# Two-layer cross-attention: the first batch's scores start ahead of the layer-1 weight preparation, which moves into that batch's layer 0

## The chip, the cores and the metric

The kernel runs on one core of a Trainium2 chip. The metric is the device time of one execution in microseconds; the time before is the median of three runs, 1359.41 us (1356.07 to 1359.81).

## The reference, cut to what matters

There are 16 batches. Each has 100 query rows `x` and 361 context rows `ctx_2048`, both 512 wide, all in float32. Two layers follow each other and both attend to the same context.

```
layer 0:  q = x@Wq + bq; k = ctx@Wk + bk; v = ctx@Wv + bv      # 32 query heads of 16, 8 key/value heads
          attn = softmax(q k^T / 4 + mask0)
          x = layernorm(attn v @ Wo + bo + x) * gamma + beta
layer 1:  a = layernorm(ctx) * ln_gamma + ln_beta              # mean and variance of each context row
          Q = x@Wq^T; K = a@Wk^T; V = a@Wv^T                   # 16 heads of 32
          attn = softmax(Q K^T / sqrt(32)), masked
          x = x + tanh(gate) * (attn V @ Wo^T)
```

The layer norm of the context is folded into the layer-1 weights: Wk and Wv of layer 1 are multiplied by ln_gamma, their column means are subtracted (centring), and the keys are then scaled by each context row's reciprocal deviation. ln_beta gives a bias per column. This folding is done once, before or during the first batch.

## The kernel before, in words

**Engines.** One block holds a program for each engine: SP issues all transfers in order on one queue, PE does matmuls and transposes, DVE, ACT and POOL the rest. They meet only through semaphores. Each program is written out by hand, so the order of the lines is the order of the work on that engine.

**A batch.** There are 48 heads in all, handled in 24 pairs p. Pairs 0 to 15 are layer 0, pairs 16 to 23 layer 1. For a head k, `score` (L387, L391) is one matmul into bank k % 3 of SCO, `shift` on DVE (L752) adds the mask and finds the row's minimum, `exps` on ACT (L962) makes the probabilities. The score of head k waits for the exponentials of head k - 3 (`prob` at least k - 2). Two pairs later `transpose_probs` (L401) transposes a pair into TP, and ACT (three of four pairs, L975) or DVE (one of four, L765) copies them to PT. `out_half` (L421, L426) multiplies with the values.

**Layer-1 keys and values of a batch** are spread between the pairs. `keys1` is 48 matmuls in four chunks m of twelve (weights in a high and a low part), into PJ. A chunk then goes by `keys1_scaled` on DVE (L744), an addition of the bias on POOL (L1130), `keys1_high` on ACT (L992), and a subtraction on POOL (L1133). SP stores it with `store_keys1` (L253) and, when two chunks are stored, reads them back in another layout with `load_keys1` (L260, four transfers into K1S). `keys1_high` of chunks 2 and 3 waits until the store of chunks 0 and 1 has landed. `values1` is 36 matmuls into PJ.

**What a batch loads for the next one.** At the head of its loop SP runs, in this order: `load_keys1(b, 0)`, the next batch's XT (L297), the next AT (L211), a wait for POOL's mask step (`mk1_a`), the mask MU (L303), the next batch's context rows into V1, also called NAT (L216, L218), and then `store_keys1` of chunks 2 and 3. POOL's mask step (L1157) stands behind `keys1_low(b, 2)` in POOL's program. DVE takes statistics of the next batch's context rows (`ctx_stats`, L730) in pair 9, behind its two shifts and `repeat_sums`, and in pair 10; its first one waits for the two row transfers (`l_nat`). V1 is then overwritten by the values of the batch, from ACT's pair 11.

**The prologue.** After layer-0 keys, queries and values of batch 0 (L350, L363, L380), PE does the layer-1 key bias (L499), the column means of the key weights (L504), the value bias (L509), the value weights' means (L515), and then 36 of the 48 `keys1` matmuls (`K1_AHEAD`). DVE centres the key weights (L823), makes their low part (L827), adds the layer-0 value bias (L721) and centres the value weights (L835). ACT makes the high parts (L1026, L1030) and POOL the low part of the value weights (L1149). Only then does `batch(0, True, True)` begin with the first score (L387), which waits for Q0S and K0S (L239, L245). The raw key weights lie in the first half of PT, the raw value weights in the second, so the first copies into PT wait for both low parts.

**Names that the change touches**: `WK1_raw`, `K1_STEPS`, `V1_STEPS`, `keys1_scaled`, `keys1_high`, `keys1_low`, and the order of SP, PE, DVE, ACT and POOL up to and in batch 0. Batches 1 to 15 keep their order.

Of the kernel before, what the change touches and what calls it, by code (L numbers as in the profile page):

```python
# [21 lines left out]
def two_layer_cross_attention(nc, x_rows, x_cols, ctx_rows, ctx_cols, mask0, mask1,  # L22
# [24 lines left out]
    with ExitStack() as ctx:  # L47
# [62 lines left out]
        YT = OT  # L110
        WK1_raw = PT_flat[:, 0:C * D].rearrange("p (c n) -> p c n", c=C)
        WV1_raw = PT_flat[:, WV1_AT:WV1_AT + C * D].rearrange("p (c n) -> p c n", c=C)
# [70 lines left out]
        K1_STEPS = {p: (i + K1_AHEAD, j + K1_AHEAD) for p, (i, j) in K1_LATE.items()}  # L183
        V1_STEPS = spans({3: 2, 4: 2, 5: 4, 8: 2, 9: 2, 10: 4, 11: 4, 12: 4, 13: 4, 14: 4, 15: 4})
        OUT1_STEPS = {6: (0, 2), 7: (2, 5), 8: (5, 8)}
        PV0_PARTS = {7: (0, 0, 2), 9: (0, 2, 3), 11: (1, 0, 2), 12: (1, 2, 3), 15: (2, 0, 2)}
# [22 lines left out]
        def _(sp):  # L209
# [61 lines left out]
            load_ctx_rows(0)  # L271
            sp.dma_start(PT_flat[:, 0:C * D], wk1.rearrange("p c n -> p (c n)")).then_inc(l_k1, 16)
            sp.dma_start(ROWS[:, :], rows.partition_broadcast(P)).then_inc(l_row, 16)
# [5 lines left out]
            sp.dma_start(MU[0:T, :], mask1[0].partition_broadcast(T)).then_inc(l_mk1, 16)  # L279
            sp.dma_start(R0[0:T, :], x_rows[0]).then_inc(l_xn, 16)  # L280
            for G in range(2):
                for j in range(NJ):
                    ct, jh = 2 * (j % 2) + G, j // 2
                    sp.dma_start(WO0[32 * ct:32 * ct + 32, 2 * jh:2 * jh + 2, :],
                                 wo0[32 * j:32 * j + 32, 2 * G:2 * G + 2, :]).then_inc(l_o, 16)
            sp.wait_ge(wk_c, C)
            sp.dma_start(WQ1[:, :, :], wq1).then_inc(l_o, 16)
            sp.wait_ge(wv_c, C)
# [51 lines left out]
        def _(pe):  # L340
# [162 lines left out]
            for c in range(C):  # L503
                last = pe.matmul(SCO[:, 0, :], ONES[:, :], WQ1[:, c, :], start=c == 0, stop=c == C - 1)  # L504
            last.then_inc(wk_cm, 1)
            pe.wait_ge(l_v1, 16)
            for m in range(C):
                for c in range(C):
                    last = pe.matmul(TP[:, 0, m:m + 1], WV1_raw[:, c, m * P:(m + 1) * P], B1[:, c:c + 1],  # L509
                                     start=c == 0, stop=c == C - 1)  # L510
            last.then_inc(kb_mm, 1)
            pe.wait_ge(wv_g, C)
            pe.wait_ge(k0_l, 1)
            for c in range(C):
                last = pe.matmul(SCO[:, 1, :], ONES[:, :], WO1[:, c, :], start=c == 0, stop=c == C - 1)  # L515
            last.then_inc(wv_cm, 1)
            pe.wait_ge(k1w_l, 1)
            for i in range(K1_AHEAD):
                if i == 3 * C:
                    pe.wait_ge(q0_l, 4)  # L520
                elif i == 6 * C:
                    pe.wait_ge(k1_f, 1)
                keys1(0, i)
            pe.wait_ge(wv_c, C)
            pe.wait_ge(kb_ev, 1)
            pe.wait_ge(vb_ev, 1)
            pe.wait_ge(rs_ev, 1)

# [6 lines left out]
            def values1_steps(b, first, p):  # L535
                for i in range(*V1_STEPS.get(p, (0, 0))):
# [12 lines left out]

            def batch(b, first, more):  # L550

                for p in range(L0P):
# [17 lines left out]
                    if p == 5 and not first:  # L570
                        pe.wait_ge(k1_f, 4 * b + 4)
                        sums_transposed(b - 1, 2)
                    keys1_steps(b, p)
                    values1_steps(b, first, p)
                    if p in OUT1_STEPS and not first:
                        if p == 6:
                            pe.wait_ge(attn, 3 * b)
                        out1(b - 1, range(*OUT1_STEPS[p]))
# [114 lines left out]
        def _(dve):  # L693
# [61 lines left out]
            def probs_out(b, p):  # L755
                dve.wait_ge(pt_mm, NPAIR * b + p + 1)
                h = p // 4
                if p == 1 and isinstance(b, int) and b == 0:
                    dve.wait_ge(k1w_l, 1)
                if p == 5 and isinstance(b, int) and b == 0:  # L760
                    dve.wait_ge(v1w_l, 1)
                if p % 4 == 1:

                    wait_from(dve, pv, NHALF * b + h - 1)
                dve.tensor_copy(PT[0:SP, h % 2, 2 * (p % 4):2 * (p % 4) + 2, :], TP[0:SP, :, 0:SC * T]).then_inc(pt_dve, 1)  # L765
# [52 lines left out]
            keys0_low(0)  # L818
            queries0_low(0)
            dve.wait_ge(kb_mm, 1)  # L820
            dve.wait_ge(wk_cm, 1)
            for c in range(C):
                dve.scalar_tensor_tensor(out=WK1_raw[:, c, :], in0=SCO[:, 0, :], scalar=-1.0 / D,  # L823
                                         in1=WQ1[:, c, :], op0=ALU.mult, op1=ALU.add)\
                    .then_inc(wk_c, 1)
            dve.wait_ge(k1w_h, 1)
            dve.tensor_tensor(flat(WK1l), PT_flat[:, 0:C * D], flat(WK1h).bitcast(F32), ALU.subtract)\  # L827
                .then_inc(k1w_l, 1)
            dve.wait_ge(pool_zero, 3)
            dve.wait_ge(l_row, 16)  # L830
            values0(0, SCO[:, 2, :])
            dve.wait_ge(wv_cm, 1)
            dve.wait_ge(kb_mm, 2)
            for c in range(C):
                dve.scalar_tensor_tensor(out=WV1_raw[:, c, :], in0=SCO[:, 1, :], scalar=-1.0 / D,  # L835
                                         in1=WO1[:, c, :], op0=ALU.mult, op1=ALU.add)\
                    .then_inc(wv_c, 1)
            dve.wait_ge(l_rp, 16)
            dve.tensor_copy(RP[:, :, :], SX[:, 0:2, :]).then_inc(rep_id, 1)
# [101 lines left out]
        def _(act):  # L941
# [23 lines left out]
            def probs_out(b, p):  # L965
                act.wait_ge(pt_mm, NPAIR * b + p + 1)
                h = p // 4
                if p == 0 and isinstance(b, int) and b == 0:
                    act.wait_ge(k1w_l, 1)
                if p == 4 and isinstance(b, int) and b == 0:  # L970
# [51 lines left out]
            act.wait_ge(kb_mm, 2)  # L1022
            act.activation(KB[:, :], TP[:, 1, 0:C], ACT.Copy).then_inc(kb_ev, 1)
            act.activation(VBC[:, :], TP[:, 0, 0:C], ACT.Copy).then_inc(vb_ev, 1)
            act.wait_ge(wk_c, C)
            act.activation(flat(WK1h), PT_flat[:, 0:C * D], ACT.Copy).then_inc(k1w_h, 1)  # L1026
            act.wait_ge(pad_zero, 3)
            rstd_out(0)
            act.wait_ge(wv_c, C)
            act.activation(flat(WV1h), PT_flat[:, WV1_AT:WV1_AT + C * D], ACT.Copy).then_inc(v1w_h, 1)  # L1030
            keys1_high(0, 0, True)
            keys1_high(0, 1, True)

            def batch(b, first, more):
                for p in range(L0P + 1):
# [12 lines left out]
                    if p == 13:  # L1048
                        unit_sums(b, 0, 2 * T)
                    if p == 2:  # L1050
                        keys1_high(b, 2, first)
                    elif p == 5:
                        keys1_high(b, 3, first)
                    elif p == 11:
# [53 lines left out]
        def _(pool):  # L1108
# [19 lines left out]
            def keys1_low(b, m):  # L1128
# [103 lines left out]
```

## Time and profile before

| | |
|---|---|
| median of 3 runs | 1359.41 us |
| profiled execution | 1352.98 us |
| its span, first to last instruction | 1351.2 us |
| PE busy | 1224.0 us, 91% of the span |
| PE weight loads | 904.3 us, 67% |
| DVE busy | 766.1 us, 57% |
| ACT busy | 766.0 us, 57% |
| POOL busy | 272.9 us, 20% |
| mean granted TensorE clock | 0.973 |
| DMA | 153.75 MB, mean 114 GB/s |
| sizes in KB: one K1S load, four transfers of | 364 |
| XT; AT; MU | 200; 722; 35.3 |
| context rows of one batch, two transfers | 484 and 238 |
| one store of a key chunk | 364 |

The durations come from the one profiled execution, whose time is 1352.98 us; it is 1.8 us over its span and 6.4 us below the median. An engine counts as busy while it has an instruction that moves data; waits, branches and the issue of transfers are not busy time. A row's bracket gives how long the engine was idle ahead of it and who ended that.

### The profile page before, as it was taken

Reading aid. Unit: us, or ns where it says so; the run is one execution under the profiler, and the core shown is the slowest. Engines: PE = TensorE matmul, PEld = TensorE weight load, DVE = VectorE, ACT = ScalarE, POOL = GpSimd, SP = SyncE. Lnnn points to the kernel's source line nnn. Section 1 sums busy time; section 2 is a strip of 40 time slices with the busy share of each in tenths; the row PEclk is TensorE's granted clock in tenths of the full one; section 3 lists DMA queues with packets and bytes.
Section 4 is the critical chain, followed back from the end, with each engine's and each line's share of the span. In section 5 each row is a group of like instructions: output and inputs, shape, how many; then the busy total and the mean of one; then the engine's idle time right before and its main releaser. Section 6 shows DMA issues by size and latency. Waiting matters only on the chain.

```text
span 1351.2 us, 31567 instructions
## 1 busy us (share of the span) xinstructions
PE 1224.0 (91%) x9768; PEld 904.3 (67%) x9768; DVE 766.1 (57%) x2289; ACT 766.0 (57%) x2179; POOL 272.9 (20%) x280
## 2 busy tenths in 40 slices
PE   4899999999999899999989999999999999999967
PEld 4666676766767667676767667677666766766645
DVE  3465646656564666556566555656656566665533
ACT  3374647566464755637475564746647465664634
POOL 2311112121221312122131211213121121212100
PEclk8899999999999999999999999999999999999986
DMA  7753735255372635537163463616347361643500
GB/s 231 192 130 89 179 65 153 70 126 131 81 178 57 161 73 112 141 76 182 51 158 76 109 156 74 172 47 158 92 93 172 74 168 44 147 110 87 129 0 7
DMA packets 77820, 153.75 MB, mean 114 GB/s; under 512 B 10384, under 2 KB 47056, under 8 KB 77152
## 3 DMA queue, kind: packets, MB, share of 16 engines
q1 hardware_dynamic: 77792, 153.40, 46.8%
q8 instruction: 15, 0.25, 0.1%
q14 instruction: 13, 0.11, 0.0%
HBM read 113.72 MB, written 39.65 MB: 114 GB/s over the span
## 4 chain that ended last, share of the span: by engine, by line
PE 71%; issue 10%; DVE 8%; ACT 7%; DMA 2%; POOL 1%; DVEq 1%; ACTq 0%; SPq 0%; POOLq 0%
PE PJ L350 16%; PE TP L401 13%; PE SCO L387 7%; PE OA L421 5%; PE PJ L451 5%; PE SCO L624 5%; PE PJ L363 4%; PE SCO L443 4%; ACT PR L962 3%; PE SCO L391 3%; PE OA L426 3%; ACT PT L975 1%; DVE SCO L752 1%; PE SCO L350 1%; POOL YRS L1169 1%
## 5 line engine op out<-in xcount | busy, mean ns | idle before, releaser
L962 ACT ACTIVATE PR<-SCO,MN 100x361 f32<-100x361 f32 x768 | 426.6, 566 | 206.9 <-DVE MN L752 205.3
L752 DVE CUSTOM_DVE_ANT_0 SCO<-SCO,MK 100x361 f32<-100x361 f32 x768 | 398.2, 553 | 223.0 <-PE SCO L387 169.9
L401 PE MATMUL TP<-ident,PR 100*128 100x100 f32 x2304 | 269.5, 253 | 9.0 <-ACT PT L975 7.0
L401 PEld LDWEIGHTS TP<-ident,PR 100*128 100x128 f32 x2304 | 237.5, 143 | 58.5 <-ACT PT L975 15.6
L975 ACT ACTIVATE PT<-TP 121x600 f32<-121x600 f32 x288 | 194.4, 675 | 86.4 <-PE TP L401 84.8
L962 ACT ACTIVATION_READ_ACCUMULATOR PR<-SCO,MN 100x1 f32 x768 | 158.1, 206 | 0.0
L387 PE MATMUL SCO<-K0S,Q0S 64*100 64x362 f32 x512 | 130.2, 411 | 5.9 <-ACT PR L962 5.9
L765 DVE COPY PT<-TP 121x600 f32<-121x600 f32 x96 | 75.2, 783 | 104.4 <-PE TP L401 103.5
L391 PE MATMUL SCO<-K1S,Q1S 128*100 128x362 f32 x256 | 94.1, 402 | 23.3 <-ACT PR L962 18.5
L752 DVE DVE_READ_ACCUMULATOR2_ANT MN<- 100x1 f32 x768 | 108.8, 142 | 0.0
L451 PE MATMUL PJ<-WO,OT 128*100 128x256 f32 x256 | 70.4, 412 | 27.7 <-DVE OT L787 27.7
L350 PE MATMUL PJ<-TH,WK1h 128*128 128x364 f32 x256 | 93.9, 367 | 1.2 <-DVE WK1l L827 0.9
L1133 POOL TENSOR_TENSOR K1HL<-K1F,K1HL 128x364 fp32r<-128x364 f32 x64 | 61.6, 963 | 157.2 <-ACT K1HL L992 153.4
L421 PE MATMUL OA<-PT,V0P 121*32 121x200 f32 x1536 | 91.5, 350 | 0.8 <-ACT PT L975 0.8
L387 PEld LDWEIGHTS SCO<-K0S,Q0S 64*100 64x100 f32 x512 | 55.2, 161 | 48.8 <-ACT PR L962 15.4
L350 PE MATMUL PJ<-WV1h,TH 128*121 128x512 f32 x192 | 80.9, 422 | 6.7 <-DVE R L794 6.7
L350 PE MATMUL PJ<-TL,WK1h 128*128 128x364 f32 x256 | 86.2, 337 | 0.0
L350 PE MATMUL PJ<-TH,WK1l 128*128 128x364 f32 x256 | 84.3, 329 | 0.0
L1130 POOL TENSOR_TENSOR K1F<-K1F,KB 128x364 f32<-128x364 f32 x64 | 50.9, 795 | 154.0 <-DVE K1F L744 154.0
L350 PE MATMUL PJ<-WV1h,TL 128*121 128x512 f32 x192 | 81.9, 426 | 0.0
L350 PE MATMUL PJ<-WV1l,TH 128*121 128x512 f32 x192 | 81.6, 425 | 0.0
L1163 POOL TENSOR_TENSOR R<-R,ROWS 100x512 f32<-100x512 f32 x16 | 20.6, 1288 | 278.5 <-DMA R<-x_rows 278.5
(138 smaller groups left out, 1781.9 us busy)
## 6 DMA issues: line engine op xcount, KB each, us to landing
K1S<-k_scr SPq DMA_DIRECT2D x128, 364.0 KB, 6.2
k_scr<-K1HL SPq DMA_DIRECT2D x64, 364.0 KB, 2.5
Q0S<-q_scr SPq DMA_DIRECT2D x128, 100.0 KB, 3.9
K0S<-k_scr SPq DMA_DIRECT2D x64, 182.0 KB, 4.9
AT<-ctx_cols SPq DMA_DIRECT2D x16, 722.0 KB, 9.4
V<-ctx_rows SPq DMA_DIRECT2D x16, 484.0 KB
q_scr<-QHL SPq DMA_DIRECT2D x16, 400.0 KB, 2.5
k_scr<-KHL SPq DMA_DIRECT2D x32, 182.0 KB, 3.0
```

The source lines that it names most:

```text
L350: return pe.matmul(dst, w, x, start=start and term == 0, stop=stop and term == 2)
L387: pe.matmul(dst, Q0S[64 * G:64 * G + 64, j, 2 * gh + gl, :], K0S[64 * G:64 * G + 64, j, 0:SE], start=True, stop=True).then_inc(scored, 1)
L391: pe.matmul(dst, Q1S[:, j, m, :], K1S[:, j, m, 0:SE], start=True, stop=True).then_inc(scored, 1)
L401: last = pe.transpose(TP[:, k % 2, c * T:(c + 1) * T], PR[0:T, k % NPR, c * SP:c * SP + P], ident[0:T, 0:T])
L421: last = pe.matmul(OA[32 * j:32 * j + 32, 0:2 * T], lhs, rhs, start=gh == 0 and c == 0, stop=gh == 1 and c == SC - 1)
L451: last = pe.matmul(PJ[0:T, 1, cols], OT[:, c, :], WO1[:, c, cols], start=c == 0, stop=c == C - 1)
L624: last = pe.matmul(SCO[:, 1, m * T:(m + 1) * T], WQ1[:, c, m * P:(m + 1) * P], YT[:, c, :], start=c == 0, stop=c == C - 1)
L752: dve.tensor_tensor_reduce(out=bank, in0=bank, in1=mask[0:T, :], scale=scale, scalar=3.4e38, op0=ALU.add, op1=ALU.min, accum_out=MN[0:T, k ...
L765: dve.tensor_copy(PT[0:SP, h % 2, 2 * (p % 4):2 * (p % 4) + 2, :], TP[0:SP, :, 0:SC * T]).then_inc(pt_dve, 1)
L962: act.activation(PR[0:T, k % NPR, 0:S], SCO[0:T, k % 3, 0:S], ACT.Exp, bias=MN[0:T, k:k + 1], scale=-1.0, accum_out=SM[0:T, k:k + 1]).then ...
L975: act.activation(PT[0:SP, h % 2, 2 * (p % 4):2 * (p % 4) + 2, :], TP[0:SP, :, 0:SC * T], ACT.Copy).then_inc(pt_act, 1)
L1133: pool.tensor_tensor(K1HL[:, m % 2, 1, :], K1F[:, :], K1HL[:, m % 2, 0, :].bitcast(F32), ALU.subtract).then_inc(k1_l, 1)
```

## The change

The raw key weights go to WO0, so the first half of PT is free at once; WO0's own eight loads move behind the key weights' low part, and WQ1's load goes ahead of them. The means go to PJ and not to SCO. The first scores are issued right after the key weights' means. Value bias, value means, low parts, all 48 key matmuls and their scaling, high and low parts come between the pairs of batch 0. Cut to its core:

```diff
-        WK1_raw = PT_flat[:, 0:C * D].rearrange("p (c n) -> p c n", c=C)
+        WK1_raw = WO0
+        FIRST_K1_STEPS = spans({2: 7, 3: 7, 4: 7, 5: 7, 6: 7, 7: 7, 8: 6})
+        FIRST_V1_STEPS = spans({9: 6, 10: 6, 11: 6, 12: 6, 13: 6, 14: 4, 15: 2})
 # SP
+            sp.wait_ge(wk_c, C)
+            sp.dma_start(WQ1[:, :, :], wq1).then_inc(l_o, 16)
+            sp.wait_ge(k1w_l, 1)
             for G in range(2):
                 for j in range(NJ):
...
-            sp.wait_ge(wk_c, C)
-            sp.dma_start(WQ1[:, :, :], wq1).then_inc(l_o, 16)
             sp.wait_ge(wv_c, C)
             sp.dma_start(WO1[:, :, :], wo1).then_inc(l_o, 16)
             store_keys1(0, 0)
 # PE
-                last = pe.matmul(SCO[:, 0, :], ONES[:, :], WQ1[:, c, :], start=c == 0, stop=c == C - 1)
+                last = pe.matmul(PJ[:, 0, :], ONES[:, :], WQ1[:, c, :], start=c == 0, stop=c == C - 1)
             last.then_inc(wk_cm, 1)
...
-            pe.wait_ge(k1w_l, 1)
-            for i in range(K1_AHEAD):
...
+            def first_keys1_steps(p):
+                for i in range(*FIRST_K1_STEPS.get(p, (0, 0))):
+                    if i == 0:
+                        pe.wait_ge(k1w_l, 1)
+                    elif i == 3 * C:
+                        pe.wait_ge(wv_c, C)
+                    elif i == 6 * C:
+                        pe.wait_ge(k1_f, 1)
+                    elif i == 9 * C:
+                        pe.wait_ge(k1_f, 2)
+                    keys1(0, i)
...
-                    keys1_steps(b, p)
+                    if first:
+                        first_keys1_steps(p)
+                    else:
+                        keys1_steps(b, p)
                     values1_steps(b, first, p)
+                    if first and p == 0:
+                        values1_bias()
+                    elif first and p == 1:
+                        pe.wait_ge(q0_l, 4)
+                        values1_means()
+                    elif first and p == 2:
+                        pe.wait_ge(kb_ev, 1)
+                        pe.wait_ge(vb_ev, 1)
+                        pe.wait_ge(rs_ev, 1)
 # DVE: values0 and the copy to RP now stand ahead of the centring of the key weights
-                if p == 1 and isinstance(b, int) and b == 0:
-                    dve.wait_ge(k1w_l, 1)
-            keys1_scaled(0, 0)
-            keys1_scaled(0, 1)
...
-                    if p == 0:
+                    if first and p in (4, 6, 8, 10):
+                        keys1_scaled(b, p // 2 - 2)
+                    elif not first and p == 0:
                         keys1_scaled(b, 2)
-                    elif p == 4:
+                    elif not first and p == 4:
                         keys1_scaled(b, 3)
                     for k in (2 * p, 2 * p + 1):
                         shift(b, k)
+                    if first and p == 0:
+                        keys1_weights_low()
+                    elif first and p == 1:
+                        values1_centred()
 # ACT: the high part of the key weights stays ahead of the first exponentials
-            keys1_high(0, 0, True)
-            keys1_high(0, 1, True)
...
-                    if p == 2:
-                        keys1_high(b, 2, first)
-                    elif p == 5:
-                        keys1_high(b, 3, first)
+                    if first and p == 1:
+                        act.wait_ge(kb_mm, 2)
+                        act.activation(VBC[:, :], TP[:, 0, 0:C], ACT.Copy).then_inc(vb_ev, 1)
+                    elif first and p == 3:
+                        act.wait_ge(wv_c, C)
+                        act.activation(flat(WV1h), PT_flat[:, WV1_AT:WV1_AT + C * D], ACT.Copy).then_inc(v1w_h, 1)
+                    elif first and p in (5, 7, 9, 11):
+                        keys1_high(b, (p - 5) // 2, first)
+                    elif not first and p == 2:
+                        keys1_high(b, 2, first)
+                    elif not first and p == 5:
+                        keys1_high(b, 3, first)
 # POOL
-            keys1_low(0, 0)
-            keys1_low(0, 1)
             pool.wait_ge(v1w_h, 1)
             pool.tensor_tensor(flat(WV1l), PT_flat[:, WV1_AT:WV1_AT + C * D], flat(WV1h).bitcast(F32), ALU.subtract)\
                 .then_inc(v1w_l, 1)
+            keys1_low(0, 0)
+            keys1_low(0, 1)
```

## Rows read from the trace of the kernel before

**Rows 1.** The page's chain that ended last, share of the span, by engine.
```profile
PE 71%; issue 10%; DVE 8%; ACT 7%; DMA 2%; POOL 1%; DVEq 1%; ACTq 0%; SPq 0%; POOLq 0%
```

**Rows 2.** PE's timeline, 40 to 100 us: start, duration, [idle before, releaser].
```profile
40.89 3.63 PE L509 MATMUL TP<-COLS,PT 128*128 128x1 f32 x32
44.38 3.68 PE L515 MATMUL SCO<-WO,ONES 128*128 128x512 f32 x8
48.97 0.43 PE L350 MATMUL PJ<-TH,WK1h 128*128 128x364 f32 x1 [0.91 <-DVE WK1l L827]
...
55.12 0.41 PE L387 MATMUL SCO<-K0S,Q0S 64*100 64x362 f32 x2
55.86 0.43 PE L350 MATMUL PJ<-TH,WK1h 128*128 128x364 f32 x1 [0.34 <-DVE K1F L744]
...
60.17 0.62 PE L387 MATMUL SCO<-K0S,Q0S 64*100 64x362 f32 x1 [2.88 <-ACT PR L962]
...
81.63 0.41 PE L387 MATMUL SCO<-K0S,Q0S 64*100 64x362 f32 x2
...
83.35 0.40 PE L350 MATMUL PJ<-WV1h,TH 128*121 128x512 f32 x1
...
99.22 1.22 PE L421 MATMUL OA<-PT,V0P 121*32 121x200 f32 x24
```

**Rows 3.** Stretches of 4 us: engines' busy us, granted clock, DMA share, GB/s.
```profile
60.00:64.00 4.00, 3.83 (x11) 2.73 (x12) 1.91 (x7) 2.35 (x10) 3.48 (x2) 0.50 0.60 148
64.00:68.00 4.00, 4.00 (x21) 2.68 (x19) 2.08 (x7) 2.96 (x10) 2.62 (x3) 0.67 1.04 210
68.00:72.00 4.00, 3.50 (x22) 2.36 (x20) 2.69 (x10) 2.91 (x9) 1.48 (x2) 1.00 1.05 286
72.00:76.00 4.00, 3.21 (x35) 1.99 (x33) 2.54 (x9) 3.75 (x12) 1.50 (x2) 1.00 0.91 250
```

**Rows 4.** DVE's timeline, 40 to 80 us, same columns as rows 2.
```profile
41.16 2.48 DVE L823 SCALAR_TENSOR_TENSOR PT<-SCO,WQ 128x512 f32<-128x512 f32 x4 [17.39 <-PE SCO L504]
46.62 2.29 DVE L827 TENSOR_TENSOR WK1l<-PT,WK1h 128x2048 fp32r<-128x2048 f32 x1 [2.97 <-ACT WK1h L1026]
...
49.30 2.47 DVE L835 SCALAR_TENSOR_TENSOR PT<-SCO,WO 128x512 f32<-128x512 f32 x4
...
79.24 0.69 DVE L730 BATCH_NORM_STATS2 CST<-V 121x6 f32<-121x512 f32 x1
```

**Rows 5.** POOL's timeline, 55 to 66 us, same columns.
```profile
57.30 0.95 POOL L1133 TENSOR_TENSOR K1HL<-K1F,K1HL 128x364 fp32r<-128x364 f32 x1 [0.62 <-ACT K1HL L992]
58.21 4.52 POOL L1149 TENSOR_TENSOR WV1l<-PT,WV1h 128x2048 fp32r<-128x2048 f32 x1
62.68 0.80 POOL L1130 TENSOR_TENSOR K1F<-K1F,KB 128x364 f32<-128x364 f32 x1
```

**Rows 6.** SP's timeline of issues, 35 to 67 us: start, time to issue.
```profile
35.31 0.88 SPq L245 DMA_DIRECT2D K0S<-k_scr  x2
...
60.82 1.76 SPq L260 DMA_DIRECT2D K1S<-k_scr  x4
...
63.15 0.59 SPq L211 DMA_DIRECT2D AT<-ctx_cols  x1
...
66.51 0.37 SPq L218 DMA_DIRECT2D V<-ctx_rows  x1
```

**Rows 7.** Issue to landing: K0S, 20 to 60 us; then AT issued at 63.15.
```profile
DMA to landing us min/median/max: 4.2/4.6/5.5
...
DMA to landing us min/median/max: 11.7/11.7/11.7
```

**Rows 8.** The page's groups of an exponential: busy, mean ns of one.
```profile
L962 ACT ACTIVATE PR<-SCO,MN 100x361 f32<-100x361 f32 x768 | 426.6, 566 | 206.9 <-DVE MN L752 205.3
...
L962 ACT ACTIVATION_READ_ACCUMULATOR PR<-SCO,MN 100x1 f32 x768 | 158.1, 206 | 0.0
```

**Rows 9.** The page's transfers by form: count, KB each, median us to landing.
```profile
k_scr<-K1HL SPq DMA_DIRECT2D x64, 364.0 KB, 2.5
```

More of the change, by code:

```diff
@@ L271, in _ @@
             load_ctx_rows(0)
-            sp.dma_start(PT_flat[:, 0:C * D], wk1.rearrange("p c n -> p (c n)")).then_inc(l_k1, 16)
+            sp.dma_start(WK1_raw[:, :, :], wk1).then_inc(l_k1, 16)
             sp.dma_start(ROWS[:, :], rows.partition_broadcast(P)).then_inc(l_row, 16)
@@ L503, in _, with values1_bias, values1_means @@
             for c in range(C):
-                last = pe.matmul(SCO[:, 0, :], ONES[:, :], WQ1[:, c, :], start=c == 0, stop=c == C - 1)
+                last = pe.matmul(PJ[:, 0, :], ONES[:, :], WQ1[:, c, :], start=c == 0, stop=c == C - 1)
             last.then_inc(wk_cm, 1)
-            pe.wait_ge(l_v1, 16)
-            for m in range(C):
-                for c in range(C):
[L509 to L516, printed above, removed]
-            pe.wait_ge(k1w_l, 1)
-            for i in range(K1_AHEAD):
[L519 to L527, printed above, removed]
+            def values1_bias():
+                pe.wait_ge(l_v1, 16)
+                for m in range(C):
+                    for c in range(C):
+                        last = pe.matmul(TP[:, 0, m:m + 1], WV1_raw[:, c, m * P:(m + 1) * P], B1[:, c:c + 1],
+                                         start=c == 0, stop=c == C - 1)
+                last.then_inc(kb_mm, 1)
+            def values1_means():
+                pe.wait_ge(wv_g, C)
+                for c in range(C):
+                    last = pe.matmul(PJ[:, 1, :], ONES[:, :], WO1[:, c, :], start=c == 0, stop=c == C - 1)
+                last.then_inc(wv_cm, 1)
+            def first_keys1_steps(p):
[9 more added lines that the diff above has]
+                    keys1(0, i)
             def keys1_steps(b, p):
@@ L535, in values1_steps @@
             def values1_steps(b, first, p):
-                for i in range(*V1_STEPS.get(p, (0, 0))):
+                for i in range(*(FIRST_V1_STEPS if first else V1_STEPS).get(p, (0, 0))):
                     if i == 0:
@@ L819, in _ @@
             queries0_low(0)
+            dve.wait_ge(pool_zero, 3)
+            dve.wait_ge(l_row, 16)
+            values0(0, SCO[:, 2, :])
+            dve.wait_ge(l_rp, 16)
+            dve.tensor_copy(RP[:, :, :], SX[:, 0:2, :]).then_inc(rep_id, 1)
             dve.wait_ge(kb_mm, 1)
@@ L822, in _, with keys1_weights_low, values1_centred @@
             for c in range(C):
-                dve.scalar_tensor_tensor(out=WK1_raw[:, c, :], in0=SCO[:, 0, :], scalar=-1.0 / D,
+                dve.scalar_tensor_tensor(out=WK1_raw[:, c, :], in0=PJ[:, 0, :], scalar=-1.0 / D,
                                          in1=WQ1[:, c, :], op0=ALU.mult, op1=ALU.add)\
                     .then_inc(wk_c, 1)
[L826 to L839, printed above, removed]
-            keys1_scaled(0, 0)
-            keys1_scaled(0, 1)
+            def keys1_weights_low():
+                dve.wait_ge(k1w_h, 1)
+                dve.tensor_tensor(flat(WK1l), flat(WK1_raw), flat(WK1h).bitcast(F32), ALU.subtract)\
+                    .then_inc(k1w_l, 1)
+            def values1_centred():
+                dve.wait_ge(wv_cm, 1)
+                dve.wait_ge(kb_mm, 2)
+                for c in range(C):
+                    dve.scalar_tensor_tensor(out=WV1_raw[:, c, :], in0=PJ[:, 1, :], scalar=-1.0 / D,
+                                             in1=WO1[:, c, :], op0=ALU.mult, op1=ALU.add)\
+                        .then_inc(wv_c, 1)
             def batch(b, first, more):
@@ L967, in probs_out @@
                 h = p // 4
-                if p == 0 and isinstance(b, int) and b == 0:
-                    act.wait_ge(k1w_l, 1)
                 if p == 4 and isinstance(b, int) and b == 0:
@@ L1021, in _ @@
                     .then_inc(wv_g, 1)
[L1022 to L1026, printed above, removed]
             act.wait_ge(pad_zero, 3)
             rstd_out(0)
-            act.wait_ge(wv_c, C)
-            act.activation(flat(WV1h), PT_flat[:, WV1_AT:WV1_AT + C * D], ACT.Copy).then_inc(v1w_h, 1)
-            keys1_high(0, 0, True)
-            keys1_high(0, 1, True)
+            act.wait_ge(kb_mm, 1)
+            act.activation(KB[:, :], TP[:, 1, 0:C], ACT.Copy).then_inc(kb_ev, 1)
+            act.wait_ge(wk_c, C)
+            act.activation(flat(WK1h), flat(WK1_raw), ACT.Copy).then_inc(k1w_h, 1)
             def batch(b, first, more):
@@ L1049, in batch @@
                         unit_sums(b, 0, 2 * T)
-                    if p == 2:
+                    if first and p == 1:
[7 more added lines that the diff above has]
+                    elif not first and p == 2:
                         keys1_high(b, 2, first)
-                    elif p == 5:
+                    elif not first and p == 5:
                         keys1_high(b, 3, first)
-                    elif p == 11:
+                    if p == 11:
                         if more:
```

## The prediction
> **What bounds the kernel now.** I read the chain of waits first: PE holds 71% of it [rows 1], so what counts is when PE gets its next work. Then PE's timeline of the first 100 us, because nothing after batch 0's layer 0 is edited. The reader is to see there that PE is already full between the key means and the first score: the gap of 0.91 us ahead of the first key matmul is the only one from 40.9 to the score at 55.12 [rows 2]. Work that is moved behind the scores is therefore not removed. What is empty is short: 0.91, 0.34 and 2.88 us in these rows, and two gaps of 0.50 and 0.79 further on; 5.4 us in all. After the 2.88 us idle ahead of 60.17 the granted clock is 0.50 of full in 60 to 64 us and 0.67 in 64 to 68, that is 1.2 GHz for most of 6.6 us, with PE busy all that time [rows 3]: 3.0 us lost of at most 3.3. The most that the change can give is 5.4 + 3.0 = 8.4 us. Last I read SP's issues and the DMA rate, since the order of the key chunks sets when SP may go on.
>
> **The change, part by part.**
>
> The scores. The key means end where DVE's centring starts, 41.16 [rows 4]. K0S's last issue is at about 35.8 [rows 6] and lands 4.2 to 5.5 us later, 40.0 to 41.3 [rows 7]. So scores 0 and 1 stand at 41.2, 14 us earlier. The work in those 14 us comes back between the pairs: value bias 3.63, value means 3.68 [rows 2], 36 key matmuls in the 6.1 us from 48.97 to 55.12. Bank PJ for SCO costs nothing: PJ has no other use there. WO0 as the landing place costs nothing: its own loads go out at about 48 and are wanted at 100.
>
> Pairs 0 to 9. DVE centres to 43.6, shifts 0 and 1, waits for ACT's high part (2.97 us after the centring [rows 4]; two small copies are no longer in it, so 2.0) and makes the low part, 2.29, to 48.0. Shifts 2 and 3 end at 49.1 and their exponentials (0.57 + 0.21 us each less overlap, 0.75 [rows 8]) at 50.1. PE has bias to 45.5, means 46.7 to 50.4, scores 4 and 5, seven key matmuls. DVE's value centring, 2.47 [rows 4], runs 50.5 to 52.9 ahead of shifts 4 and 5 and delays score 7 by about 1.3 us. ACT's high part of the value weights delays score 9 by as much. POOL then makes the low part, 4.52 [rows 5], 57.5 to 62.0, and only then adds the bias to key chunk 0 (0.80); ACT's copy of it, queued behind exponentials 8 and 9, ends at 63.4, POOL's subtraction (0.95) at 64.4, and DVE, which waits for it in pair 6, scales chunk 1 at 64.5. A pair is then some 2.9 us of PE work (two scores, seven key matmuls at 0.17, transposes, the value products). Chunk 1: ACT's copy in pair 7 to 68.1, POOL to 69.1. Pair 9's shifts end at 73.8 and the two small sums at 74.4; score 22, which stood at 81.6 [rows 2], would stand at 78.9. By then 12 of 36 value matmuls are done where it had been 16; four more at 0.40 or less, overlapping, are 1.0 us. Up to here the change is 2.7 - 1.0 = 1.7 us ahead.
>
> The transfers. This is what decides. SP loads half the keys only when chunks 0 and 1 are stored, and behind that in its queue stand XT, AT, the mask and the next batch's context rows. Before, chunk 1 was ready at 58.25 [rows 5], the K1S load went out at 60.82, AT at 63.15, the rows to 66.9 [rows 6]. DVE took the first statistics at 79.24 without a wait [rows 4]: 18.4 us after the K1S load's start. Now chunk 1 is ready at 69.1; with the 2.6 us from ready to load as before (a store's median landing is 2.5 [rows 9]) the K1S load starts at 71.7. The rows go out at 76.2 to 76.9, since the mask step of POOL that SP waits for stands behind chunk 2, which ACT copies in pair 9. DVE wants them at 74.4, before they are even issued.
>
> When do they land? K1S, XT, AT and the mask are 4 x 364 + 200 + 722 + 35 = 2413 KB, with the rows 3135 KB. From 60 to 72 us the queue moved 4 x (148 + 210 + 286) = 2576 KB, and 250 GB/s after it [rows 3]: the first sum is passed near 71.4, the second near 74.2, or 10.6 and 13.4 us after the K1S load's start; the K1S part runs at some 210 GB/s. AT landed at 63.15 + 11.7 = 74.9, 14.1 us after it [rows 6, 7]. So the rows landed between 10.6 + 1 (some landing) and 18.4 us after it; I take 14.5, next to AT, hence 86.2 now (83.3 to 90.1).
>
> A rule that bears on it is in the Trainium skill, DMA: Bandwidth & Descriptors, section Queues, rings and completion order: each DMA engine takes its descriptors in ring order, but completion isn't first in, first out over a whole transfer. It speaks against this change: rows issued behind K1S wait for K1S's bytes. AT's landing of 11.7 us agrees, where that many KB alone would need 2 to 3 us at the rates of the rows. If the rows passed the rest, as the rule leaves open for transfers on fewer engines, they would land some 4 us after their issue; that is a rival below.
>
> DVE is in order: behind the first statistics wait the scaling of chunk 3, shifts 20 and up. PE can issue score 22 (its bank waits for exponential 19), then stands at score 23, which wants exponential 20. From 86.2: statistics 0.69, scaling 0.5, shift 20 0.5, exponential 0.7: score 23 at 88.5. PE is idle from 79.2 to 88.5, 9.3 us, and after that the clock falls as it did after 2.88 us: 3.0 us more. From score 23 to the end of the layer's transposes, 99.2, was 17.3 us of PE work without a gap [rows 2]. New end: 88.5 + 17.3 + 1.0 + 3.0 = 109.8 against 99.2: **10.6 us later**. XT (behind K1S), MK0, the second K1S load (chunk 3 scaled at 87, loaded by 103, wanted about 18 us after the layer's end) hide behind this. Batches 1 to 15 start later by the same sum and keep their pace.
>
> Profiled execution: 1352.98 + 10.6 = 1363.6 us. The median of before is 6.4 us above that execution, so the same step gives 1359.41 + 10.6 = **1370.0 us**.
>
> **Bounds.** The landing alone is -2.9 to +3.9 us. The clock's loss is 0 to 3.3. The pairs before, where ACT, DVE and POOL hand over chunk by chunk, may be 2 us quicker or 4 us slower; a slower pair moves the K1S load and the need for the rows together, so only its own length counts. Together +5 to +17.
>
> **The rivals.**
> - *Short stall.* The rows pass the K1S bytes and land 4 us after issue, at 80.9 instead of 86.2. For it: the DMA share falls only after 76 us, so no row shows which transfer ended when. Against: AT's 11.7 us. 10.6 - 5.3 = +5.3, with the clock kept +3: about 1364.
> - *Faster, on the other side.* PE's early gaps vanish and DVE never waits in pair 9. It decides if the rows land before DVE's last shift of pair 9; then the 1.7 us stays and, if the handovers of pairs 3 to 6 are smoother than mine, up to the 8.4 of the ceiling: 1351 to 1358, say 1357.5. For it: scores start 14 us earlier and only 5.4 us of gaps stood in the way. Against: POOL's 4.52 us ahead of chunk 0, and a K1S load that would have to start near 60 while its first chunk is not scaled before 57.
> - *Two stalls.* The handovers in pairs 4 to 8 also leave PE idle for long enough that the clock falls there: in those 17 us one more fall is 3.0 and its gaps 3 to 4; 10.6 + 6.5 = +17, 1376.5.
> - *It doesn't do what it says.* K0S landing late holds the first score to 41.3 at most; 0.1 us, left out.
>
> **How the numbers follow.** Long stall 65%, own range 1364.5 to 1376; short stall 14%; faster or even 11%; two stalls 10%. A measurement of this kernel can tell 0.3%, 4.1 us, from no change. The long stall and two stalls are slower, 75%; the short one is slower two times in three, 9%, else the same, 5%; the last case is half the same, 5%, half faster, 6%. Sum: faster 0.06, same 0.10, slower 0.84. The range leaves out most of the last case and the top: 1359 to 1377.
>
> **What would show it.** The first score near 41 and the first statistics of batch 1's rows as a DVE instruction with a wait on the row transfers of 7 to 15 us, in pair 9; the K1S load at 70 to 74 on SP, the rows at 75 to 79. PE idle 7 to 11 us ahead of one score of pair 11, released by ACT's exponential, then a granted clock of 0.5. The layer's last products near 110. The forecast is wrong if that DVE wait is under 3 us, if the K1S load goes out before 65, or if the later batches' period changes.

## The result: 0.6 to 1.0% slower, as forecast, by a longer wait than forecast

| | median us | runs | ratio to the kernel before, 95% interval |
|---|---|---|---|
| before | 1359.01 | 4 | |
| changed | 1368.42 | 4 | 1.0063 (1.0033 to 1.0094) |
| changed, again, in the second set of runs (before: 1353.56, 18 runs) | 1370.25 | 6 | 1.0104 (1.0072 to 1.0136) |

The forecast was 1370.0 us. The ratio is worked out from the single runs and is not quite that of the two medians. The median of before has one run more here than the 1359.41 us that the forecast started from. The two profiled executions are 1352.98 and 1361.74 us, with spans of 1351.2 and 1359.9 us.

The page of the changed kernel has its head and its chain all but unchanged against [rows 1]; the change can't be read there:

```profile
span 1359.9 us, 31565 instructions
...
PE 70%; issue 10%; DVE 8%; ACT 6%; DMA 2%; POOL 2%; DVEq 1%; ACTq 0%; SPq 0%; POOLq 0%
```

PE's timeline of the changed kernel, 40 to 115 us, with the columns of [rows 2]:

```profile
42.36 0.41 PE L390 MATMUL SCO<-K0S,Q0S 64*100 64x362 f32 x2 [0.66 <-issue]
42.69 3.73 PE L514 MATMUL TP<-COLS,PT 128*128 128x1 f32 x32
46.36 1.09 PE L390 MATMUL SCO<-K0S,Q0S 64*100 64x362 f32 x2
47.38 5.05 PE L521 MATMUL PJ<-WO,ONES 128*128 128x512 f32 x8
...
56.19 0.40 PE L390 MATMUL SCO<-K0S,Q0S 64*100 64x362 f32 x1 [1.21 <-ACT PR L987]
...
78.96 0.40 PE L390 MATMUL SCO<-K0S,Q0S 64*100 64x362 f32 x1
91.73 0.62 PE L390 MATMUL SCO<-K0S,Q0S 64*100 64x362 f32 x1 [12.37 <-ACT PR L987]
...
112.80 1.22 PE L424 MATMUL OA<-PT,V0P 121*32 121x200 f32 x24
```

The first scores stand at 42.36 in place of 55.12, and score 22 at 78.96 in place of 81.63. Then PE is idle for 12.37 us ahead of score 23, and layer 0 of batch 0 ends at 112.80 in place of 99.22 [rows 2], 13.6 us later (taken here and below at the start of its last row of products). The bracket names an exponential of ACT, which is only the last link. One line of the changed kernel's waits, 38 to 115 us (who waited for whom, us in total, times, longest), names the first:

```profile
ACT PR L987 <- DVE MN L771: 29.6, 9, 13.7
...
PE SCO L390 <- ACT PR L987: 14.5, 3, 12.4
DVE CST L749 <- DMA V<-ctx_rows: 14.1, 1, 14.1
```

DVE's timeline of the changed kernel in pairs 9 and 10 (the first statistics had no bracket in [rows 4]):

```profile
74.95 0.29 DVE L793 COPY SX<-RSM 100x256 f32<-100x256 f32 x1
89.36 0.69 DVE L749 BATCH_NORM_STATS2 CST<-V 121x6 f32<-121x512 f32 x1 [14.11 <-DMA V<-ctx_rows]
89.97 0.52 DVE L763 TENSOR_TENSOR K1F<-PJ,RSB 128x364 f32<-128x364 f32 x1
90.41 0.53 DVE L771 CUSTOM_DVE_ANT_0 SCO<-SCO,MK 100x361 f32<-100x361 f32 x1
```

The reader is to see the queue: the statistics of batch 1's rows wait, and the shift that PE's next score depends on stands behind them. SP's issues, against [rows 6]:

```profile
73.06 1.76 SPq L262 DMA_DIRECT2D K1S<-k_scr  x4
...
75.40 0.59 SPq L213 DMA_DIRECT2D AT<-ctx_cols  x1
...
77.57 0.37 SPq L220 DMA_DIRECT2D V<-ctx_rows  x1
```

and POOL's steps that set when they may go out, against [rows 5]:

```profile
59.21 4.58 POOL L1173 TENSOR_TENSOR WV1l<-PT,WV1h 128x2048 fp32r<-128x2048 f32 x1 [31.14 <-ACT WV1h L1073]
63.73 0.81 POOL L1156 TENSOR_TENSOR K1F<-K1F,KB 128x364 f32<-128x364 f32 x1
...
69.53 0.97 POOL L1159 TENSOR_TENSOR K1HL<-K1F,K1HL 128x364 fp32r<-128x364 f32 x1 [1.90 <-ACT K1HL L1015]
```

The stretches around the stall, with the columns of [rows 3] (after the stretch: PE, PE weight loads, DVE, ACT, POOL, clock, DMA share, GB/s):

```profile
80.00:84.00 4.00, 0.00 (x0) 0.00 (x0) 0.00 (x0) 0.00 (x0) 0.00 (x0) 1.00 1.04 271
84.00:88.00 4.00, 0.00 (x0) 0.00 (x0) 0.00 (x0) 0.00 (x0) 0.00 (x0) 0.53 0.84 237
88.00:92.00 4.00, 0.27 (x1) 0.24 (x1) 2.64 (x8) 0.97 (x3) 0.79 (x1) 0.50 0.19 70
92.00:96.00 4.00, 4.00 (x22) 2.36 (x22) 1.78 (x9) 2.84 (x9) 2.19 (x2) 0.50 0.19 71
96.00:100.00 4.00, 4.00 (x26) 2.70 (x25) 1.78 (x5) 0.95 (x3) 0.00 (x0) 0.76 0.08 26
```

From 80 to 88 us no engine works; only DMA does. PE comes back at 91.7 with the clock at 0.50, 1.2 GHz, and keeps it until about 98.

**Where 13.6 us became 8.8.** The starts of the result transfers split each execution in three: up to batch 0's result, the middle (the 14 results after that), and the last batch.

| profiled execution | batch 0's result | middle | last batch |
|---|---|---|---|
| before | 163.36 | 1112.9 | 72.0 |
| changed | 177.04 | 1112.5 | 67.4 |
| before, again | 165.45 | 1112.6 | 74.0 |
| changed, again | 178.13 | 1112.8 | 75.1 |

The last two of SP's issues in the changed kernel show how the table is read, 1356.99 - 1289.56 = 67.4:

```profile
1289.56 0.31 SPq L334 DMA_DIRECT2D out<-R  x1
1356.99 0.30 SPq L338 DMA_DIRECT2D out<-R  x1
```

The shift is in the first column, 13.7 and 12.7 us. The middle is the same within 0.4 us. The last batch is the same program in all four rows and takes 67.4 to 75.1 us: in the changed kernel's first profile PE ran its last products at full clock (granted 1.00 from 1348 us on), in the profile of before mostly at 1.2 GHz (0.65 from 1335 on). That this is chance and no work of the change shows in a kernel without any of it: `before_rows_late`, below, has a last batch of 67.4 us too. So one pair of profiled executions understates the shift by 4.6 us. The second set's 1.0104, 14.1 us of 1353.56, stands nearer to the trace than the first set's 1.0063, 8.6 us of 1359.01.

### The profile page after: what moved, and what is told of

It is laid out like the page before. It is cut to its first block, busy times and chain, and to the rows that moved or that the text cites. A ratio compares the mean times of both kernels' runs of the same rounds, so it can differ in the third digit from the quotient of the medians.

```text
span 1359.9 us, 31565 instructions
## 1 busy us (share of the span) xinstructions
PE 1221.9 (90%) x9768; PEld 902.3 (66%) x9768; DVE 765.5 (56%) x2289; ACT 765.0 (56%) x2179; POOL 273.0 (20%) x280
## 4 chain that ended last, share of the span: by engine, by line
PE 70%; issue 10%; DVE 8%; ACT 6%; DMA 2%; POOL 2%; DVEq 1%; ACTq 0%; SPq 0%; POOLq 0%
PE PJ L353 16%; PE TP L404 13%; PE SCO L390 7%; PE OA L424 5%; PE PJ L454 5%; PE SCO L643 5%; PE PJ L366 4%; PE SCO L446 4%; ACT PR L987 3%; PE SCO L394 3%; PE OA L429 3%; POOL YRS L1195 1%; ACT PT L998 1%; DVE SCO L771 1%; PE SCO L353 1%
## 5 line engine op out<-in xcount | busy, mean ns | idle before, releaser
L782 DVE COPY PT<-TP 121x600 f32<-121x600 f32 x96 | 75.1, 782 | 110.1 <-PE TP L404 109.2
L454 PE MATMUL PJ<-WO,OT 128*100 128x256 f32 x256 | 67.6, 399 | 27.7 <-DVE OT L804 27.7
```

The source lines that it names most:

```text
L454: last = pe.matmul(PJ[0:T, 1, cols], OT[:, c, :], WO1[:, c, cols], start=c == 0, stop=c == C - 1)
```

## The experiments

**The changed kernel once more**, unedited, in a second set of runs, on one chip with the next kernels:

> The changed kernel unedited, beside the others on one chip. The trace showed the layer 13.6 us later but the profiled executions only 8.8 us apart, since PE's clock fell differently in the last batch. If that is chance, the ratio comes out between 1.007 and 1.010 (9.5 to 13.6 us); if the changed kernel truly gets time back at the end, it stays at 1.006 or below.

The ratio is 1.0104 (1.0072 to 1.0136), a hair above the range. The last batch took 75.1 us here, so the changed kernel gets nothing back at its end: the first profile's 67.4 was chance.

**Are the late rows the loss, or the work between the pairs?** `rows_first` has the edit

```diff
+            sp.wait_ge(c_st, 3)
+            load_ctx_rows(1)
             store_keys1(0, 0)
             store_keys1(0, 1)
...
-                wait_from(sp, pv, NHALF * b)
-                sp.wait_ge(c_st, 3 * b + 3)
-                load_ctx_rows(b + 1)
+                if not first:
+                    wait_from(sp, pv, NHALF * b)
+                    sp.wait_ge(c_st, 3 * b + 3)
+                    load_ctx_rows(b + 1)
```

> The changed kernel, but batch 1's context rows are issued in SP's prologue, behind WO1 and ahead of the first key store, so near 55 us. My theory (the loss is DVE's wait of 14.1 us for these rows in pair 9): the wait is gone, PE's idle 12.4 us ahead of score 23 and the low clock after it are gone, layer 0 of batch 0 ends near 97.5 us where it was 99.2 before and 112.8 changed; the time is 1 to 3 us below the kernel before. Rival (the weight and key work between the pairs costs by itself, the wait only hides it): the layer ends at 102 or later and the time stays 3 us or more above the kernel before.

Measured: 1347.33 against 1353.56 us, ratio 0.9954 (0.9931 to 0.9977). DVE's timeline of `rows_first` and, in a second fence, PE's:

```profile
77.37 0.69 DVE L752 BATCH_NORM_STATS2 CST<-V 121x6 f32<-121x512 f32 x1
```

```profile
99.47 0.71 PE L427 MATMUL OA<-PT,V0P 121*32 121x200 f32 x12
```

There is no wait, and the layer ends at 99.47, 14.4 us ahead of the changed kernel run on the same chip beside it (113.84). It doesn't end at the forecast 97.5: PE had the slow clock from 59 to 66 us here and over the value means ahead of that. The loss was the wait. What is left of the change, with the rows out of the way, is faster than the kernel before. Repeated in a third set of runs:

> rows_first unedited, beside best on one chip and for a second estimate. If its gain is real, the ratio is again 0.993 to 0.998; if the first was chance of the clock in single batches, it is 0.998 to 1.002.

1346.53 us against 1358.58, ratio 0.9921 (0.989 to 0.9953), a little below the range that I gave; the gain is real, its size 0.5 to 0.8%.

**Is the early issue of the rows a gain of its own?** `before_rows_first` is the same SP edit in the kernel before.

> The kernel before, with the early row issue of rows_first alone (rows of batch 1 behind WO1 in SP's prologue). The rows had never been late there, so on my theory nothing changes: ratio 0.997 to 1.003. If the early rows were worth something by themselves (less crowding behind the K1S load), it would be 0.995 like rows_first, and the gain of rows_first would not belong to the early scores.

Ratio 0.9999 (0.9973 to 1.0026). It is not; the gain of `rows_first` needs the moved scores and weight work as well.

**Does the wait alone make the loss?** `before_rows_late` moves the rows in the kernel before, batch 0 only (that their old place is left out in batch 0 is as in `rows_first` and isn't printed again, here and in the next kernel):

```diff
                 load_keys1(b, 1)
+                if first:
+                    sp.wait_ge(c_st, 3)
+                    load_ctx_rows(1)
```

> The kernel before, with nothing of the change, but in batch 0 the rows are issued behind the second K1S load, near 82.5 us in place of 66. On my theory the wait alone makes the loss: rows land 93 to 95 us, DVE waits 13 to 16 us in pair 9, layer 0 ends 13 to 16 us later and the ratio is 1.008 to 1.013, like the changed kernel's. If PE had other work to fill the wait, or if the changed kernel's loss came from its spread weight work, the ratio stays under 1.004.

Ratio 1.0075 (1.0045 to 1.0106), 10.2 us, a little below the 1.008 that I gave as the least. SP's, DVE's and PE's timelines:

```profile
81.08 1.75 SPq L260 DMA_DIRECT2D K1S<-k_scr  x4
...
83.30 0.36 SPq L218 DMA_DIRECT2D V<-ctx_rows  x1
```

```profile
94.23 0.69 DVE L734 BATCH_NORM_STATS2 CST<-V 121x6 f32<-121x512 f32 x1 [8.93 <-DMA V<-ctx_rows]
```

```profile
96.16 0.62 PE L391 MATMUL SCO<-K0S,Q0S 64*100 64x362 f32 x1 [8.16 <-ACT PR L966]
...
115.78 1.22 PE L425 MATMUL OA<-PT,V0P 121*32 121x200 f32 x24
```

The rows went out at 82.9 to 83.7 and landed at 94.2, as forecast. The wait is 8.9 us and not 13 to 16, because DVE itself came later to its statistics, at 85.3: 6.1 us after the first trace of before (79.24) and 3.9 after `before_again` (81.37), whose prologue was that much earlier (K1S load at 61.48 against 65.42). Against `before_again`, whose layer ends at 101.34, the end is 14.4 us later, or 10.5 us without the prologue's part: the 8.9 us of waiting and the slow clock behind it. None of the changed kernel's work is in this kernel, and the loss is there. The second trace of the kernel before:

> The kernel before, unedited, for a second trace of it. On my theory its layer 0 of batch 0 ends where the first trace had it, 99 to 101 us, DVE's first statistics in pair 9 have no wait for the rows, and its time differs from the first profiled execution only by PE's clock in single batches.

1356.7 us, one run. Its first statistics at 81.37 have no wait. The end at 101.34 is 0.3 us beyond the 99 to 101 that I gave: after the gap ahead of its fourth score the clock stayed slow for longer than in the first trace.

**What makes the rows land late?** The prediction put it down to the bytes in front of them on the queue. Two kernels change the order of batch 0's transfers: `rows_behind_k1s` issues the rows right behind the first K1S load, ahead of XT, AT and the mask wait:

```diff
                 load_keys1(b, 0)
+                if first:
+                    sp.wait_ge(c_st, 3)
+                    load_ctx_rows(1)
```

`k1s_last` has

```diff
                 wait_from(sp, scored, NH * b - 8)
-                load_keys1(b, 0)
+                if not first:
+                    load_keys1(b, 0)
...
                 load_ctx_rows(b + 1)
+                if first:
+                    load_keys1(0, 0)
```

> The changed kernel, but in batch 0 SP issues the rows right behind the first K1S load, ahead of XT, AT and the mask wait, near 75 us. If the bytes in front of the rows on the queue set their landing: only K1S's 1456 KB stand in front (about 7 us at 210 GB/s), the rows land near 84 and DVE waits about 9 us in place of 14.1, layer end near 108, time some 5 us below the changed kernel. If the late issue behind POOL's mask step is what counts, the 2.5 us of earlier issue take 2.5 us off the wait: 11.5 us.

> The changed kernel, but in batch 0 SP issues XT, AT, mask and rows first and the K1S load behind the rows. The rows are still issued near 77 us, behind POOL's mask step. If the bytes in front count: only 957 KB are there and mostly landed by 78, so the rows land near 81 and DVE waits about 6 us; the layer ends near 105, time 7 to 8 us below the changed kernel. If the issue time alone counts, the wait stays at 14 us.

`rows_behind_k1s`: 1.0076 (1.0042 to 1.011). `k1s_last`: 1.0105 (1.007 to 1.0139). DVE's row of each, in this order:

```profile
89.14 0.69 DVE L753 BATCH_NORM_STATS2 CST<-V 121x6 f32<-121x512 f32 x1 [12.77 <-DMA V<-ctx_rows]
```

```profile
87.96 0.69 DVE L752 BATCH_NORM_STATS2 CST<-V 121x6 f32<-121x512 f32 x1 [12.48 <-DMA V<-ctx_rows]
```

Both of my figures for the bytes in front were wrong, 9 and 6 us, and so were those for the issue time alone, 11.5 and 14. The layer ends at 111.67 and 110.63, where 108 and 105 were forecast (113.84 in the changed kernel beside them). In `k1s_last` XT and AT had landed (AT issued at 71.54, 5.9 us to landing) when the rows went out at 77.4 to 78.1, and the rows still took 10.2 us from the start of their second issue, 77.79. In `rows_behind_k1s` they took 12.9 from 76.22. So I took the K1S load behind the rows away as well, in `rows_alone`:

```diff
                 load_ctx_rows(b + 1)
                 if first:
+                    sp.wait_ge(l_nat, 64)
                     load_keys1(0, 0)
```

> k1s_last with one more wait: SP issues the first K1S load only when the rows have landed. k1s_last showed rows landing 10 us after their issue with XT and AT already landed, so the bytes in front don't explain it. Theory A (the K1S transfers issued right behind them take their share of the DMA engines): alone the rows land 4 to 6 us after issue, near 83 us, and DVE waits about 7 us. Theory B (the two row transfers take about 10 us by themselves, on few engines): landing and wait are unchanged, 88 us and 12 us.

```profile
84.03 0.69 DVE L753 BATCH_NORM_STATS2 CST<-V 121x6 f32<-121x512 f32 x1 [8.97 <-DMA V<-ctx_rows]
```

The second row transfer was issued at 77.36 and the rows landed 6.7 us later. The layer ends at 106.70. The time was 1363.49 us, one run. DMA moved little but the rows meanwhile; the stretches of `rows_alone`, then of `k1s_last`:

```profile
78.00:80.00 2.00, 1.17 (x9) 0.71 (x7) 0.00 (x0) 0.00 (x0) 0.00 (x0) 1.00 0.36 73
80.00:82.00 2.00, 0.00 (x0) 0.00 (x0) 0.00 (x0) 0.00 (x0) 0.00 (x0) 1.00 0.65 205
82.00:84.00 2.00, 0.00 (x0) 0.00 (x0) 0.00 (x0) 0.00 (x0) 0.00 (x0) 1.00 0.28 102
```

```profile
80.00:82.00 2.00, 0.00 (x0) 0.00 (x0) 0.00 (x0) 0.00 (x0) 0.00 (x0) 1.00 0.93 222
82.00:84.00 2.00, 0.00 (x0) 0.00 (x0) 0.00 (x0) 0.00 (x0) 0.00 (x0) 1.00 1.08 198
84.00:86.00 2.00, 0.00 (x0) 0.00 (x0) 0.00 (x0) 0.00 (x0) 0.00 (x0) 0.64 1.05 163
```

The time from the second row issue to landing, one trace each:

| kernel | in front of the rows | behind them | us |
|---|---|---|---|
| `rows_alone` | mask (35 KB), the rest landed | nothing | 6.7 |
| `k1s_last` | mask (35 KB), the rest landed | K1S load, store of chunk 2 | 10.2 |
| `before_rows_late` | K1S load, from 81.08 | nothing | 10.9 |
| changed | K1S load, XT, AT, mask | store of chunk 2 | 11.8 |
| `rows_behind_k1s` | K1S load | XT, AT, mask, store of chunk 2 | 12.9 |

Alone they take 6.7 us, a little over theory A's 4 to 6 and well short of theory B's 10. So half of the time is the rows' own. The K1S load costs them about as much from behind, 3.5 us (with one store of 364 KB beside it), as from in front, 4.2. That fits transfers in flight that share what moves them, whichever was issued first, which is theory A. Whether they share DMA engines or the memory's side wasn't tried and is open.

**Is there more in the early start?** `best` is `rows_first` with the key bias in PE's gap near 23 us and the value bias ahead of the scores. DVE makes the key weights' low part ahead of the first shift (not printed):

```diff
-            pe.wait_ge(l_id, 16)
-            values0_transposed(0, SCO[:, 2, :])
-            rstd_rows(0)
             pe.wait_ge(l_k1, 16)
...
             last.then_inc(kb_mm, 1)
+            pe.wait_ge(l_id, 16)
+            values0_transposed(0, SCO[:, 2, :])
...
             last.then_inc(wk_cm, 1)
+            rstd_rows(0)
...
+            values1_bias()
...
                     if first and p == 0:
-                        values1_bias()
-                    elif first and p == 1:
                         pe.wait_ge(q0_l, 4)
                         values1_means()
```

> rows_first, and the value bias no longer between the pairs: PE does the key bias as soon as the key weights land (near 22.5 us, in a gap), then the layer-0 value transposes, the key means, the reciprocal deviations and the value bias, all ahead of the first scores; the value means come in pair 0 and DVE makes the key weights' low part ahead of the first shift. My theory (PE bounds pairs 0 to 10, and in rows_first the clock falls in pairs 1 to 4): 3.7 us of bias leave the pairs and some 2 us of slow clock with them, layer 0 of batch 0 ends 4 to 6 us earlier than in rows_first, ratio to the kernel before 0.989 to 0.993. Rival (K0S's landing or the handovers DVE to ACT to POOL bound the pairs): the ratio is that of rows_first, 0.995.

1346.74 us, ratio 0.9921 (0.9891 to 0.9951), the same as `rows_first_again` beside it. PE's timeline of `best`:

```profile
22.92 4.75 PE L501 MATMUL TP<-COLS,WO 128*128 128x1 f32 x32 [1.55 <-DMA WO<-wk]
...
41.50 0.62 PE L393 MATMUL SCO<-K0S,Q0S 64*100 64x362 f32 x2 [3.57 <-DMA K0S<-k_scr]
42.05 5.58 PE L523 MATMUL PJ<-WO,ONES 128*128 128x512 f32 x8
...
95.33 1.22 PE L427 MATMUL OA<-PT,V0P 121*32 121x200 f32 x24
```

The layer ends 3.3 us earlier than in `rows_first_again` (98.67), short of my 4 to 6. PE now waits 3.57 us for K0S, as the rival said, and the clock falls in that gap and is low for the means behind it. The ratio lies in the range that I gave, but so does that of `rows_first_again`, so it doesn't speak for my theory. The times don't show the 3.3 us: six runs can't tell it from the clock's chance, in the last batch above all. Both versions are faster than both kernels of the case.

**What pulls the clock down in pairs 0 to 2?** `swap` exchanges the value bias and the value means of `rows_first`; ACT's copy of the bias comes a pair later (not printed).

```diff
                     if first and p == 0:
-                        values1_bias()
-                    elif first and p == 1:
                         pe.wait_ge(q0_l, 4)
                         values1_means()
+                    elif first and p == 1:
+                        values1_bias()
```

> rows_first with the value means in pair 0 and the value bias in pair 1 (ACT's copy of it one pair later). In rows_first the granted clock fell during or after the bias, 32 matmuls of one column each with PE shown busy all the time. If such matmuls don't hold the clock up, the means now take 3.7 us in place of 5.5 and the fall comes after the bias, in pair 2; the time is within 0.2% of rows_first. If the fall came from the idle gap ahead of score 0, the means in pair 0 are slow too, over 5 us.

```profile
43.12 3.70 PE L524 MATMUL PJ<-WO,ONES 128*128 128x512 f32 x8
...
47.99 0.40 PE L393 MATMUL SCO<-K0S,Q0S 64*100 64x362 f32 x1 [0.83 <-ACT PR L990]
48.32 6.35 PE L517 MATMUL TP<-COLS,PT 128*128 128x1 f32 x32
```

```profile
48.00:52.00 4.00, 4.00 (x22) 3.83 (x22) 2.72 (x5) 1.67 (x6) 0.00 (x0) 0.63 0.64 243
52.00:56.00 4.00, 4.00 (x18) 3.67 (x19) 1.22 (x3) 0.17 (x1) 0.00 (x0) 0.50 0.65 183
```

The means are fast in pair 0, so a gap ahead of score 0 isn't the cause. The clock falls during the bias, earlier than the pair 2 that I gave, with PE shown busy all 4 us of each stretch. But it falls at about 49.1, 0.7 us into the bias and 1.1 us after the end of a gap of 0.83 us ahead of score 3; `swap` alone can't tell the bias from this gap. `rows_first` can: there PE has no gap between 29 us and the fall near 45.7, which comes 2.3 us into the bias (43.43 to 48.28). Its stretches, and below them the first trace of the kernel before, whose bias ran from 40.89 to 44.38:

```profile
44.00:46.00 2.00, 2.00 (x19) 2.00 (x18) 2.00 (x4) 0.21 (x1) 0.00 (x0) 0.93 0.00 0
46.00:48.00 2.00, 2.00 (x11) 2.00 (x11) 1.02 (x5) 2.00 (x2) 0.00 (x0) 0.50 0.64 111
```

```profile
40.00:44.00 4.00, 4.00 (x32) 3.49 (x30) 2.48 (x4) 0.00 (x0) 0.00 (x0) 1.00 1.05 235
44.00:48.00 4.00, 4.00 (x13) 1.79 (x12) 1.38 (x1) 2.40 (x4) 0.00 (x0) 1.00 0.93 299
```

So the clock can fall with PE shown busy throughout, and in most of the traces it falls during the bias or within 1.5 us behind it; but the same 32 matmuls don't always bring it down. The time of `swap`, 0.9962 (0.9941 to 0.9983), is 0.4% above `rows_first_again` beside it, more than my 0.2%. Its slow clock lasts from 49 to 59 us, over the bias and the next scores, and its layer ends at 100.97, 2.3 us later; the rest of the difference isn't traced.

## Why the prediction was right, step by step

- *Scores at 41.2.* At 42.36; the key means ended later than in the first trace. The transfers were no hindrance (K0S held PE only in `best`).
- *Pairs 0 to 9, 1.7 us ahead at score 22.* Forecast 78.9 and measured 78.96, 2.67 us ahead less 1.0 for the value matmuls. That it is right within 0.1 us is in part luck. The handovers are those that were worked out, but each came late: DVE's value centring at 52.5 (50.5), POOL's low part 59.2 to 63.8 (57.5 to 62.0), chunk 1 ready at 70.5 (69.1), DVE's sums done at 75.2 (74.4). Later pairs were shorter than assumed and made it up. One cost stands nowhere in the sum: the clock fell in these pairs too, over the value means (5.05 us for 3.68) and again from 57 to 60, of the kind that *two stalls* described, at less than its price. PE's gap of 1.2 us at score 7 is there; the one forecast for score 9 isn't, and one of 0.87 stands at score 13.
- *The K1S load at 71.7, rows issued 76.2 to 76.9.* At 73.1 and 77.2 to 77.9.
- *The rows land at 86.2.* At 89.4, inside 83.3 to 90.1 but 3.2 us late: the load started 1.4 us late, and the rows landed 16.3 us after its start in place of 14.5. This is the mis-sized term, and the reason given for it was the weaker part of the text. I had the rows wait for the bytes in front. With all but the mask's 35 KB landed (`k1s_last`) they still took 10.2 us. The sign in favour was misread too: AT's 11.7 us were set against 2 to 3 us for that many KB alone, but with only XT ahead AT took 5.9 us in `k1s_last`. The estimate held because it was taken from the same sequence of transfers in the trace, not because its mechanism was right, and within that, 14.5 was a choice in a range of 11.6 to 18.4. By the same token the rival *short stall*, 4 us from issue to landing, was out of reach: even alone the rows take 6.7.
- *DVE's order turns this into PE's idle time.* Right: a wait of 14.1 us (11.8), score 23 at 91.73 (88.5), PE idle 12.37 us (9.3). `before_rows_late` shows that the wait suffices.
- *The clock costs 3.0 us after it.* The stretch from score 23 to 112.80 is 21.1 us where 17.3 stood: 3.8 for the clock and the four more value matmuls, where 4.0 was forecast.
- *The sum.* 13.6 us in the trace in place of 10.6. The first median's 9.4 us is nearer to the forecast than the trace is, through the clock in the last batch; the second set of runs gives 14.1.
- *Faster, on the other side.* This rival's point of decision was right (rows landed before DVE's last shift of pair 9): once `rows_first` meets it, the kernel is 0.5 to 0.8% faster, 6 to 11 us, at and beyond the top of the 8.4 that I called the ceiling. The traces show less: the layer ends at 99.47 and 98.67 where the two traces of the kernel before and the one of `before_rows_first` have 99.22, 101.34 and 104.02, and batch 0's result goes out at 162.2 and 161.4 against 163.4, 165.5 and 166.6. Part of the rest is the clock: the mean granted clock of the runs is 0.974 in both sets of `rows_first` and 0.970 and 0.968 in the kernel before beside them. An estimate from a straight line through the times of each set against that clock, read at 0.970, leaves 2.2 us of gain in the second set and 4.1 in the third. Why the runs of `rows_first` have the higher clock is not shown.

## What to carry to other kernels

Before work is moved later in one stage, list what is issued behind it on the transfer queue, and for whom: here a load for the next batch stood behind a store of the moved work, and its reader stood in an in-order engine ahead of the critical path. A load whose buffer is free should be issued then, not where the loop's body has it; that one move turned 0.6 to 1.0% of loss into 0.5 to 0.8% of gain. (To move the reader behind the shifts in DVE's program would be another cure; it wasn't tried.) For a transfer's landing take the same sequence of transfers out of a trace, since a sum of the bytes in front gave the wrong answer when the order changed.

## What the runs showed of the hardware that was not expected

- Transfers issued behind another one on the same queue slow it: the two row transfers, 722 KB, took 6.7 us alone (`rows_alone`) and 10.2 us with the K1S load, 1456 KB, and a store of 364 KB issued behind them (`k1s_last`), in one trace each. With 1456 KB in front and nothing behind they took 10.9 us (`before_rows_late`).
- A PE shown busy without a gap can lose its clock during 32 matmuls of one column each: in `rows_first` the granted clock goes from 0.93 (44 to 46 us) to 0.50 (46 to 48 us) with PE at 2.00 of 2.00 us in both. It isn't certain: in the first trace of the kernel before it stays at 1.00 over the same matmuls. Where it falls behind them, the eight 512-column instructions that follow take 5.05 us (the changed kernel) in place of 3.68 [rows 2].
- The last batch of one program takes between 67.4 and 76.4 us over thirteen profiled executions, with a mean granted clock in it of 0.82 at the short end and 0.69 at the long end, while the 14 batches' middle stays at 1112.5 to 1114.3 us. A single pair of profiles can't size a change of a few us; the position of one landmark in each, as the layer's end here, can.
